# A twelve-stage Perceiver kernel: another order in the quantised feed-forward, a transfer issued one group later, and idle TensorE products added in eight stages

## The reference, cut to what matters

```python
def act_qdq(x):
    qmax = 2.0 ** (ACT_BITS - 1) - 1.0
    scale = jnp.maximum(jnp.max(jnp.abs(x)) / qmax, 1e-12)
    return jnp.clip(jnp.round(x / scale), -qmax - 1.0, qmax) * scale

def fixed_qdq_u16(x):
    scale = 1.0 / 65536.0
    return jnp.clip(jnp.round(x / scale), 0.0, 65535.0) * scale

def lpbq_dequant(w):
    O, I = w.shape
    qmax = 2.0 ** (W_BITS - 1) - 1.0
    wb = w.reshape(O, I // BLOCK, BLOCK)
    s = jnp.maximum(jnp.max(jnp.abs(wb), axis=-1, keepdims=True) / qmax, 1e-12)
    wq = jnp.clip(jnp.round(wb / s), -qmax - 1.0, qmax) * s
    return wq.reshape(O, I)
```

## Time and profile before

| what | value |
|---|---|
| median of three runs | 1528.3 us (1526.83 to 1528.82) |
| the profiled execution, its own time | 1533.09 us |
| its span, first to last instruction | 1531.3 us |
| PE busy | 1441.5 us, 94% |
| PE weight loads busy | 1091.7 us, 71% |
| DVE busy | 929.9 us, 61% |
| ACT busy | 764.7 us, 50% |
| POOL busy | 80.8 us, 5% |
| mean granted TensorE clock | 0.983 |

### The profile page before, as it was taken

One profiled execution on the slowest core, in us unless ns is written; L12 is line 12 of the kernel. 1 busy time (PEld: TensorE's weight loads), 2 busy tenths in 40 slices (PEclk: granted clock), 3 DMA queues, 4 the chain that ended last, 5 costly groups with the idle time before them and its releaser, 6 DMA issues. The chain is left out here.

```text
span 1531.3 us, 29708 instructions
## 1 busy us (share of the span) xinstructions
PE 1441.5 (94%) x11418; PEld 1091.7 (71%) x11418; DVE 929.9 (61%) x2890; ACT 764.7 (50%) x1793; POOL 80.8 (5%) x78
## 2 busy tenths in 40 slices
PE   7999999998899889999999999999998798889987
PEld 6988989965677554677677767777676696666765
DVE  5755546656676432677777777777777276444434
ACT  6845445523122221567766766666677691333222
POOL 2310000000000000100000000000000000000000
PEclk9999999997999999999999999999999999999999
DMA  9935624211357299311111111100100300508760
GB/s 338 357 122 190 230 74 168 97 42 71 138 183 276 90 327 350 121 37 38 38 38 38 38 37 38 37 10 30 38 2 2 128 1 12 224 1 282 267 247 5
DMA packets 67645, 182.31 MB, mean 119 GB/s; under 512 B 5296, under 2 KB 48048, under 8 KB 65712
## 3 DMA queue, kind: packets, MB, share of 16 engines
q1 hardware_dynamic: 66352, 171.98, 31.0%
q10 hardware_dynamic: 1152, 8.42, 1.4%
HBM read 179.86 MB, written 0.52 MB: 118 GB/s over the span
## 5 line engine op out<-in xcount | busy, mean ns | idle before, releaser
L2077 ACT ACTIVATE cross_s<-cross_s,cross_shift 128x896 f32<-128x896 f32 x224 | 215.1, 1031 | 35.1 <-DVE cross_shift L2161 35.1
L2071 ACT COPY cross_eT<-cross_ring 128x512 f32<-128x512 f32 x280 | 153.1, 591 | 143.5 <-PE cross_ring L1999 143.5
L1999 PEld LDWEIGHTS cross_ring<-consts,cross_s 128*128 128x128 f32 x1568 | 169.9, 142 | 56.1 <-issue 43.4
L1999 PE MATMUL cross_ring<-consts,cross_s 128*128 128x128 f32 x1568 | 198.6, 279 | 6.3 <-ACT cross_s L2077 6.3
L2152 DVE CUSTOM_DVE_ANT_0 cross_s<-cross_scores,cross_mask,cross_top 128x448 f32<-128x448 f32 x224 | 141.3, 681 | 83.2 <-PE cross_scores L1988 83.1
L508 ACT ACTIVATE slots_probs<-slots_scores,slots_bias,ctx_rinv 128x128 f32<-128x128 f32 x294 | 130.2, 458 | 99.8 <-DVE slots_bias L551 99.8
L2152 DVE CUSTOM_DVE_ANT_0 cross_s<-cross_scores,cross_mask,cross_half_max 128x448 f32<-128x448 f32 x224 | 141.2, 680 | 16.4 <-PE cross_scores L1988 16.4
L160 PEld LDWEIGHTS slots_scores<-slots_qkT,slots_ctxT 128*128 128x128 f32 x1176 | 139.3, 195 | 9.6 <-DMA slots_ctxT<-in_ctxT 6.7
L160 PE MATMUL slots_scores<-slots_qkT,slots_ctxT 128*128 128x128 f32 x1176 | 140.6, 278 | 5.7 <-DMA slots_ctxT<-in_ctxT 5.0
L402 PE MATMUL slots_attended<-ctx_rows,slots_probs 128*128 128x257 f32 x588 | 134.0, 380 | 0.3 <-DVE slots_pooled L565 0.3
L1988 PE MATMUL cross_scores<-cross_keysT,cross_qz 32*128 32x448 f32 x896 | 118.4, 586 | 1.3 <-DVE cross_qz L2122 1.3
(11 more groups left out here) (809 smaller groups left out, 2110.2 us busy)
## 6 DMA issues: line engine op xcount, KB each, us to landing
slots_ctxT<-in_ctxT SPq DMA_DIRECT2D x39, 896.0 KB, 4.6
ctx_rows<-in_ctx_rows SPq DMA_DIRECT2D x28, 896.0 KB, 7.8
ctx_rows<-in_moe_w SPq DMA_DIRECT2D x24, 1024.0 KB, 9.9
cross_ctxT<-in_ctxT SPq DMA_DIRECT2D x13, 896.0 KB, 5.4
padded_ctxT<-in_ctxT SPq DMA_DIRECT2D x12, 896.0 KB, 4.6
plain_ctxT<-in_ctxT SPq DMA_DIRECT2D x12, 896.0 KB, 4.7
local_layers<-in_w_local SPq DMA_DIRECT2D x2, 4552.0 KB, 14.4
weights_region<-in_moe_w SPq DMA_DIRECT2D x7, 1024.0 KB, 11.2
```

The lines of the kernel that those rows point to most:

```text
L1999: last = pe.transpose(bank(("turn", u, t))[:, j * P:(j + 1) * P], s_buf[:, u % 2, j, t * P:(t + 1) * P], K.ident)
L2071: act.copy(eT[:, u % 2, t], bank(item)).then_inc(st("emptied_act"), 1)
L2077: act.activation(rows, rows, ACT.Exp, bias=shift[:, u % 2, j:j + 1], scale=SCALE).then_inc(st("exp"), 1)
```

## The change

- **slots**: ScalarE issues quant_up after group 1's exponentials in iteration 1, not after group 0's.
- **patt**: three of the 28 pieces of the weights' quantisation (Q_LATE, all of w_down) are left for the quant stage.
- **quant**: PE turns only w_gate first, runs 4 idle products, turns h, makes gate and up, runs 9 idle products, turns w_down, runs 12 more. VectorE does the three late pieces between hT and gate; it takes up's row maximum before it finishes rounding gate. The sigmoid is rounded by two Relu activations on ScalarE, whose bias operands (columns of rounds) add and subtract the rounding constant; a fused operation on VectorE clips it and multiplies it with gate. ScalarE copies w_down's lots after that.
- **padded, plain**: 2, 1 and 3 idle products around the last turn and the last two attends. **moe**: 1 and 2 near its end.
- **cross**: 5 idle products ahead of the last turn; the last spread_decay stands ahead of the last attend; one more tile of the last turn is copied by VectorE.
- **delta**: 13 idle products for 9. **mqa**: 4 idle products in the first wait, where the causal mask was written; the mask goes into the second wait, with 3 idle products for 7.

```diff
-                        if it == 1 and g == 0:
+                        if it == 1 and g == 1:
...
-Q_SPLIT = (1, 1, 1, 7, 2, 2, 2, 2, 4, 6)
+Q_LATE = ((5, 3), (6, 2), (6, 3))
+Q_SPLIT = (1, 1, 1, 7, 2, 2, 2, 2, 4, 3)
...
+                for n in range(gate_lots):
+                    copy_lot(n)
                 act.wait_ge(st("gate_ready"), 1)
                 act.activation(sig[:, :], gate[:, :], ACT.Sigmoid).then_inc(st("sigmoid"), 1)
+                act.wait_ge(st("sigmoid"), 1)
+                act.wait_ge(st("rounds"), 2)
+                act.activation(sig[:, :], sig[:, :], ACT.Relu, bias=rounds[:, 0:1], scale=SIGQ).then_inc(st("sigmoid"), 1)
+                act.wait_ge(st("sigmoid"), 2)
+                act.activation(sig[:, :], sig[:, :], ACT.Relu, bias=rounds[:, 1:2], scale=1.0 / SIGQ).then_inc(st("sigmoid"), 1)
+                for n in range(gate_lots, len(lots)):
+                    copy_lot(n)
...
+                for n in range(gate_lots):
+                    turn_lot(n)
+                idle_products(pe, K, idle_bank, 4)
                 pe.wait_ge(st("h_q"), 1)
...
-                idle_products(pe, K, tr, 38)
+                idle_products(pe, K, idle_bank, 9)
+                pe.wait_ge(st("down_quantised"), len(Q_LATE))
+                for n in range(gate_lots, len(lots)):
+                    turn_lot(n)
+                idle_products(pe, K, idle_bank, 12)
                 pe.wait_ge(st("o_q"), 1)
...
+                Quantise(st, K, "quant", "down_quantised", UP_BLOCKS, Q_PIECES, Q_LATE, only_late=True).some(dve, len(Q_LATE))
                 dve.wait_ge(st("gate_mm"), 1)
-                quantise(1, gate[:, :], mm_gate[:, 0:QFFN], "gate_ready")
+                row_max(mm_gate[:, 0:QFFN])
+                scaled(1, gate[:, :], mm_gate[:, 0:QFFN])
                 dve.wait_ge(st("up_mm"), 1)
-                quantise(2, up[:, :], mm_up[:, 0:QFFN], "up_q")
-                dve.wait_ge(st("sigmoid"), 1)
-                link(dve.tensor_scalar(sig[:, :], sig[:, :], SIGQ, ROUND, ALU.mult, ALU.add))
-                link(dve.tensor_scalar(sig[:, :], sig[:, :], ROUND, 0.0, ALU.subtract, ALU.max))
-                link(dve.tensor_scalar(sig[:, :], sig[:, :], SIGQ - 1.0, 1.0 / SIGQ, ALU.min, ALU.mult))
-                link(dve.tensor_tensor(gate[:, :], gate[:, :], sig[:, :], ALU.mult))
+                row_max(mm_up[:, 0:QFFN])
+                rounded(gate[:, :], "gate_ready")
+                scaled(2, up[:, :], mm_up[:, 0:QFFN])
+                rounded(up[:, :], "up_q")
+                dve.wait_ge(st("sigmoid"), 3)
+                link(dve.scalar_tensor_tensor(out=gate[:, :], in0=sig[:, :], scalar=(SIGQ - 1.0) / SIGQ, in1=gate[:, :],
+                                              op0=ALU.min, op1=ALU.mult))
...
+            if g == GROUPS:
+                idle_products(pe, K, free, 2)
             if 1 <= g <= GROUPS:
                 turn(g - 1)
+            if g == GROUPS + 1:
+                idle_products(pe, K, free, 1)
             if g >= 2:
                 attend(g - 2)
+        idle_products(pe, K, free, 3)
...
+                    if p == COUPLES + 1:
+                        idle_products(pe, K, turned, 1)
                     if p >= 2:
                         scatter(p - 2)
...
+                idle_products(pe, K, turned, 2)
...
-                    self.add(("turn", u - 1, t), "dve" if t in (1, 3) else "act")
+                    self.add(("turn", u - 1, t), "dve" if t in (1, 3, 5 if u == STEPS else 3) else "act")
...
-                    if u == 0 and tiles[0] == 0:
+                    if u in (0, STEPS - 1) and tiles[0] == 0:
...
+                    if u == STEPS + 1:
+                        spread_decay(GROUPS - 1)
                     if 0 <= u - 2:
                         attend(u - 2)
...
-                idle_products(pe, K, b[6], 9)
+                idle_products(pe, K, b[6], 13)
...
-                for j in range(2):
-                    pe.matmul(s_mm[:, 4 * j:4 * j + 4], K.ident, repeat(K.causal, 4), start=True, stop=False)
+                idle_products(pe, K, mm2, 4)
                 pe.wait_ge(st("ln_done"), 1)
...
-                idle_products(pe, K, mm, 7)
+                for j in range(2):
+                    pe.matmul(s_mm[:, 4 * j:4 * j + 4], K.ident, repeat(K.causal, 4), start=True, stop=False)
+                idle_products(pe, K, mm, 3)
```

More of the change, by code:

```diff
@@ L254, with __init__ @@
 class Quantise:
-    def __init__(self, st, K, name, tag, first, pieces):
+    def __init__(self, st, K, name, tag, first, pieces, late=(), only_late=False):
         self.st, self.K, self.name, self.tag, self.pieces = st, K, name, tag, pieces
@@ L261, in __init__ @@
         self.each = count // pieces
-        self.places = iter([(step, piece) for step in range(Q_STEPS) for piece in range(pieces)])
+        places = list(late) if only_late else [sp for sp in itertools.product(range(Q_STEPS), range(pieces)) if sp not in late]
+        self.signalled = {place: n + 1 for n, place in enumerate(places)}
+        self.places = iter(places)
     def some(self, dve, count):
@@ L268, in some @@
                 self.K.weights.wait(dve, self.name)
-            if step:
-                dve.wait_ge(self.st(self.tag), self.pieces * (step - 1) + piece + 1)
+            if (step - 1, piece) in self.signalled:
+                dve.wait_ge(self.st(self.tag), self.signalled[step - 1, piece])
             part = slice(piece * self.each, (piece + 1) * self.each)
@@ L904, in _ @@
                 link = linked(dve, st("vector_step"))
-                rest = Quantise(st, K, "quant", "quantised", UP_BLOCKS, Q_PIECES)
+                rest = Quantise(st, K, "quant", "quantised", UP_BLOCKS, Q_PIECES, Q_LATE)
                 stats, mv = lnb[0]
@@ L1004, in stage_quantised @@
         small = st.sb("small", [P, 4])
+        rounds = st.sb("rounds", [P, 2])
         lnb = norm_buffers(st, "ln")
@@ L1016, in stage_quantised @@
                 lots.append(([gate_n[:, o + j, c * P:(c + 1) * P] for j in range(3)], gateT[:, c, o * P:(o + 3) * P]))
+        gate_lots = len(lots)
         for i in range(QC):
@@ L1028, in _, with copy_lot @@
                 norm_scalar(act, st, "ln", lnb)
-                for n, (srcs, dst) in enumerate(lots):
+                def copy_lot(n):
+                    srcs, dst = lots[n]
                     act.wait_ge(st("lot_mm"), n + 1)
                     act.copy(dst, tr4[n % 2][:, 0:len(srcs) * P]).then_inc(st("lot_copied"), 1)
+                for n in range(gate_lots):
+                    copy_lot(n)
                 act.wait_ge(st("gate_ready"), 1)
                 act.activation(sig[:, :], gate[:, :], ACT.Sigmoid).then_inc(st("sigmoid"), 1)
+                act.wait_ge(st("sigmoid"), 1)
[5 more added lines that the diff above has]
+                    copy_lot(n)
                 root_table(act, K)
@@ L1044, in _, with turn_lot @@
             def _(pe):
-                for n, (srcs, _) in enumerate(lots):
+                def turn_lot(n):
+                    srcs, _ = lots[n]
                     if n >= 2:
@@ L1053, in _ @@
                 pe.wait_ge(st("hT"), 1)
-                pe.wait_ge(st("lot_copied"), len(lots))
+                pe.wait_ge(st("lot_copied"), gate_lots)
                 for mm, wT, done in ((mm_gate, gateT, "gate_mm"), (mm_up, upT, "up_mm")):
@@ L1081, in _ @@
                 norm_vector(dve, link, st, "ln", K.x, h[:, :], lnb)
[L1082 removed]
+                row_max(h[:, :])
+                dve.memset(rounds[:, 0:1], ROUND).then_inc(st("rounds"), 1)
+                dve.memset(rounds[:, 1:2], -ROUND / SIGQ).then_inc(st("rounds"), 1)
+                scaled(0, h[:, :], h[:, :])
+                rounded(h[:, :], "h_q")
                 dve.wait_ge(st("hT_mm"), 1)
                 dve.tensor_copy(hT[:, :], oT_mm[:, 0:D].rearrange("p (c k) -> p c k", k=P)).then_inc(st("hT"), 1)
+                Quantise(st, K, "quant", "down_quantised", UP_BLOCKS, Q_PIECES, Q_LATE, only_late=True).some(dve, len(Q_LATE))
@@ L1095, in _ @@
+                row_max(gate[:, :])
+                scaled(3, gate[:, :], gate[:, :])
+                rounded(gate[:, :], "gated_q")
                 link(dve.tensor_tensor(up[:, :], up[:, :], gate[:, :], ALU.mult))
-                quantise(4, up[:, :], up[:, :], "o_q")
+                row_max(up[:, :])
+                scaled(4, up[:, :], up[:, :])
+                rounded(up[:, :], "o_q")
                 dve.wait_ge(st("oT_mm"), 1)
@@ L1175, in attend @@
             last.then_inc(st("attended"), 1)
+        free = self.sc[GROUPS % 2]
         for g in range(GROUPS + 2):
@@ L1991, in turn @@
                 def turn(u, tiles):
-                    if u == 0 and tiles[0] == 0:
-                        ring.await_free(pe, ("turn", 0, 0))
-                        idle_products(pe, K, bank(("turn", 0, 0)), 5)
+                    if u in (0, STEPS - 1) and tiles[0] == 0:
+                        ring.await_free(pe, ("turn", u, 0))
```

(3 more changed lines are left out.)

8 lines of the change are left out of this document (5 added, 3 removed).

## The result

The changed kernel takes 1520.8 us (median of 4 runs, 1519.3 to 1524.6) against 1528.6 us beside it: ratio 0.995, 95% interval 0.993 to 0.9971. That is 7.7 us faster. 15.5 us were forecast, and 1520.8 lies just above the range of 1507 to 1520. The same kernel timed again later (e7) gave 1518.3 us against 1527.3, ratio 0.994 [0.9917, 0.9963]. So the direction is right and the size is about half of what was said.

The account below looks back on a forecast made before the run. Bound stage by stage by what each stage's end waits for, with PE busy 94%. Terms 3.7 + 1.7 + 4.7 + 2.1 + 1.6 + 2.8 − 0.3 = 16.3, less 0.8: 1528.3 − 15.5 = 1512.8, say 1513 us; range 1507 to 1520.

Parts of the forecast that it names:

- slots, 3.7: Slots: the later quant_up removes PE's 2.04 us wait for ctxT and the slow group behind it (1.7 us); 3.7 us saved.
- patt, 1.7: Patt's end: with three weight pieces moved into quant, line 986 waits for f_mm alone; 1.7 us saved.
- quant up to gate, 4.7: Quant's start: h turned 1.6 us earlier, gate product 2.75 and transposes 0.3 us shorter at full clock; 4.7 us saved.
- gate to gate times sigmoid, 2.1: Quant: three VectorE passes over the sigmoid go away and one POOL wait moves; 2.1 us saved.
- rival C: The clock falls at new places, quant's second wait and delta's start: 3 us at either, 1516 to 1519; 12 in 100.
- cross's end, 2.8: Cross's end: last turn at full clock saves 1.4 us, spread_decay ahead of the last attend 1.4 us; together 2.8.
- delta, 0: Delta: 13 idle products take 5.67 us of a wait of 5.7; no gain, at worst 0.2 us lost.
- rival A: The forecast itself: clock up through quant's start, cross's end and mqa; 1513 us, range 1508 to 1517; 62 in 100.
- Rival B: Quant starts at 0.50 all the same, as transposes don't count as busy: 4.7 us lost, 1518; 20 in 100.
- E: Quant stays at 0.50 until o and PE's own list sets its end: slower, 1532 us; 2 in 100.
- F: Quant's Relus bring table loads or VectorE's late pieces aren't hidden: 2 to 3 us, 1515; 1 in 100.
- D: Slots' stall only moves to the next group: 3 us back, 1516; 3 in 100.

Follow-up runs that it names:

- e8: Changed kernel with delta's idle products back at 9 and more idle products in waits of patt, quant, cross and delta; 1518.5 us, ratio 0.993.
- e11: Kernel before with quant's and cross's edits, 17 idle products for 12 ahead of quant's last turn, and padded's idle products; ratio 0.9941.
- e2: Kernel before with quant_up issued one group later and nothing else; ratio 1.0001.
- e6: Kernel before with the idle products of padded, folded, plain, moe and mqa alone; ratio 1.001.
- e13: Changed kernel with quant_up fetched where it was before and delta's idle products back at 9; ratio 0.9934.
- e14: Changed kernel without the idle products of padded, folded, plain, moe and mqa, and with delta's back at 9; ratio 0.9972.
- e10: Kernel before with quant's and cross's edits and none of the others; ratio 0.9976.
- e1: Kernel before with the change of patt and quant alone; ratio 0.9979.
- e3: Changed kernel with delta's idle products back at 9 from 13; 1515.7 us, ratio 0.9935.
- e9: Kernel before with cross's four edits alone; ratio 0.999.
- e12: Kernel before with the five idle products ahead of cross's last turn alone; ratio 1.0003.
- e4: Changed kernel with cross as it was before, without its four edits; 1518.4 us, ratio 0.9944.
- e15: Changed kernel with delta's idle products back at 9 and without those ahead of plain's last turn and last attend; 1517.5 us, ratio 0.993.

## Why the prediction was right in kind and twice too large

Seventeen executions were profiled in all. A stage's length here is the distance between the first layer-norm instructions of two stages (patt's begins with the issue of its first transfer). Mean, with lowest and highest and the number of profiles, sorted by whose code the stage has. The row of cross and delta runs on to the last norm inside the local layer, 70.6 us into it (72.3 in e8). The rest hardly varies: moe 55.5 to 56.1 us, the local layer behind that norm 12.2, hashed 19.3 to 19.4.

| stretch | code of before | code of after |
|---|---|---|
| slots | 312.0 (310.6 to 315.3; 9) | 311.3 (309.8 to 314.1; 8) |
| patt | 48.2 (48.0 to 49.2; 6) | 47.0 (46.3 to 48.5; 11) |
| quant | 36.1 (34.8 to 38.4; 6) | 32.0 (31.2 to 32.4; 11) |
| padded and folded | 145.9 (144.5 to 147.0; 5) | 145.6 (144.6 to 147.4; 8) |
| cross, delta, local to its last norm | 763.3 (762.9 to 764.4; 4) | 761.3 (758.9 to 765.2; 10) |
| plain | 103.0 (102.8 to 104.1; 10) | 103.4 (103.3 to 103.5; 7) |
| mqa | 25.5 (24.3 to 27.1; 9) | 24.3 (24.3 to 24.3; 8) |

The differences are −0.8, −1.2, −4.0, −0.3, −2.0, +0.5 and −1.2, which add up to −9.0 us; the two timings gave −7.7 and −9.1. Two things blur the table. "Code of after" leaves the number of idle products aside: e8's and e11's waits hold more, and eight of the ten profiles in cross's row have 9 in delta; the two with 13 have 765.2 and 759.8. And the profiled executions are single ones: e2's and e6's were the fastest of twelve, so the column of before is rather too short than too long.

Against the forecast's 15.5 us, 6.5 are missing: 2.1 in slots, 2.0 in quant up to gate, 0.8 each in quant's end and in cross with delta, 0.5 in patt, 0.5 in plain, 0.4 in mqa; padded with folded and moe's border came out 0.6 better than forecast. Term by term:

**slots, 3.7 (2.9 against the median): 0.8.** The cause of the wait was read rightly, but not all of it went: 0.90 us of 2.04 stayed in after. Over all profiles PE waits 1.95 us for ctxT around this place on the mean with the earlier transfer (1.53 to 2.54; 9) and 0.92 with the later one (0.55 to 1.54; 8), so the wait gives 1.0 us and not 2.04. The 1.7 us of the group that took 5.02 us at 0.50 are one execution's luck: of the nine profiles with this code only before has that fall. e2 and e13 show no gain in the timed runs, which can't tell 1 us.

**patt, 1.7: about 1.2.** The step is as described: f_mm ends at 364.51 and line 989 starts at 364.55. The mean is lower because the low stretches further up in patt vary from profile to profile.

**quant up to gate, 4.7: this is the step that failed.** h is turned 4.17 us after the stage's start in after and 5.68 after it in e2, where the clock was up but for the first 3.3 us: 1.5 us, the forecast's own 1.6. The 2.75 and 0.3 of clock were put on top as if the kernel before always lost them. It lost them in 2 of 6 profiles (38.4 us; the others 34.8 to 34.9), so the mean gain is 3.6 × 2/6 = 1.2, and the term measures 2.7 in place of 4.7. Six profiles are few, and as e2 and e6 are among the four, the 1.2 may be too small. The prediction did say that other executions might have kept their clock, and took off 0.8 us for slots alone; it should have asked this of every 0.50 in the earlier trace rows. The 4.8 us by which the profiled execution stood above the median were the sign: its slots and its quant alone were 2.7 and 2.4 us above the means of the table.

**gate to gate times sigmoid, 2.1: right**, 2.2 us. VectorE waited 0.23 us for the second Relu, which took 0.94 us where at most 0.92 was estimated (by size alone the row of 1.03 us gives 0.88). No table load stands between sigmoid and Relu. The Trainium skill's page "ScalarE: Activation LUTs" (Rules for kernel authors) has these passes on VectorE. Here the rows held: the passes paid on ScalarE, which had been idle for 8.83 us ahead of the sigmoid.

**quant's end, taken as 0: −1.1 in 8 of 11 profiles.** The prediction feared that PE's second list would run past o. It ended 2.45 us before o, and the clock was at 0.50 behind that wait, which is one of the two places that rival C named. In the other three folded started low instead (39.5 to 39.7 us against 36.9), 2.7 us more.

**padded and folded, 0:** kept at 0 only because the products are there. With quant changed and without them the two stages are 149.2 us long (148.3 to 150.9; 3 profiles), 3.6 us more, and e14 against e13, which differ by all those products and the transfer, is 5.6 us in the timed runs. Hence the parts don't add: e6 alone shows no gain, e10 has 0.9976, all together 0.994.

**moe's border, −0.3 and no gain in cross: 0 and about 1.** The border cost nothing that shows (moe 55.9 us either way). That a higher clock at cross's start gains nothing was wrong. The first mask still starts 9.9 to 11.1 us after the start, but cross's h is turned 6.4 us after the start in e1 and 4.7 in e3, because PE is in its key projections (6.45 us for 12 products against 4.75), and this 1.7 us is still there at the last attend: 593.4 against 590.3 us after the start, of which the last turn is the other 1.4. e9, with e3's edits and a low start, has 592.0.

**cross's end, 2.8: right.** With the same low start (e9 against before) cross is 2.85 us shorter. But e12 with five products alone reached 599.2 us and e4 without any edit 599.5, both with start and last turn at full clock. In e4 the last attend starts 590.3 us after the stage's start, as in e3: the last turn's half of the term is clock again, and only the order's half is sure.

**delta, 0: −1.0 on the mean, −5.9 in the first profile.** Rival C had this place at 3 us and 12 in 100. The first profile's 5.9 us are the 3.5 behind silu and 2.4 at the stage's end, where it had 0.50 for 13.7 us and before 6.8. In all profiles silu is through 17.5 us after the stage's start, at whatever clock. With full clock at the start and 9 products PE turns it at 17.55 (before, e1, e2, e8). At a low start it does so at 17.5 to 19.3 with 9 products and at 18.4 to 21.1 with 13. Where PE began them latest, 15.4 us after the start, 9 products had it turn at 19.3 (e6, e12) and 13 at 21.1 (after): 1.7 us is the price of the four, and the term "13 idle products take 5.67 us of a wait of 5.7" was right only at 2.4 GHz with nothing late ahead of them. Undoing this one edit (e3) gave the fastest median of all, 1515.7 us, but its interval overlaps that of 13.

**mqa, 1.6: 1.2 on the mean**, since before's code had the clock there in 3 of 9 profiles; **plain, 0: +0.5**, as the two products ahead of its last turn and the one ahead of the last attend put that attend off by 0.6 us. e15 without them has 102.84 us and mqa still at 24.26.

So what rival A wanted came up, and both places of rival C fell, at about 1 us and at up to 3.5; the forecast's own sign of being wrong, a low start of delta, was there. The sum was too large because it was made of differences between one unlucky execution and the best case of every stage. Rival B didn't happen: in none of the eleven profiles with the new quant does the stage start at 0.50, and in all six with the old one it does. The stretch of after, 365.60 to 369.80, holds idle products beside w_gate's four lots of transposes and says nothing of transposes alone. e2's does: from 363.40 to 366.60 PE ran nothing but w_gate's transposes, at 0.50, and from 366.70 it had 1.00: the clock rose on transposes alone. In before the same transposes stayed at 0.50 throughout. The Trainium skill's page "TensorE: Matmul & The Clock Gate" (Part 4: PE-mode transpose), whose rule spoke for B, says that they don't count. By e2 the trace disagrees with it again.

E and F didn't happen. D's 3 us nearly did, as slots fell short by 2.1 on the mean, but not by D's cause: the later transfer left less waiting, not the same wait elsewhere.

Left open: what decides in which of two nearly equal waits the clock falls. e3 and e15 show that neither the length of the wait nor the program decides it alone; whether the moment does at which the wait comes (it ended at 386.8 us in e3 and at 388.3 in e15) wasn't tested. What of it is the execution's and what the chip's wasn't separated either. That 13 products are worse than 9 is shown in the profiles (e6 and e12 against after) and not by the timed runs.

## What to carry to other kernels

Treat each low-clock stretch in a profile as a sample. Compare the same stage, unedited, in several executions before its recovery is counted as a gain, and price an edit of instructions at equal clock. When the profiled execution stands well above the median, its low stretches are where the excess is, and the sum from it is too large. Idle products belong to the waits around them as these are now: make the last ones end early even at half clock, and look again at the stages behind a stage that got shorter, since the products that were worth nothing before can be worth microseconds then.

## What the runs showed of the hardware

The clock first came up at some 7 to 9 us in 15 of 17 executions and at about 19 us in the two others (after and e10), with the same code, and that alone made slots 3 to 4 us longer (after 314.1 us, e7 309.8). Waits of 2.45 and 2.46 us of PE in the same code were followed by 0.50 in one execution and 1.00 in another (e3, e15). In e2 the clock rose behind 3.2 us in which PE did nothing but transposes at 0.50. A bias-and-scale Relu of 768 elements on ScalarE took 0.94 us behind a sigmoid of 0.84 us, with no table load between the two (after).
